# Node stage: the product with the attention weights and the adding of the constant row made by GpSimd for the edge sources

## The reference

```python
edge_index = jnp.stack([src, dst])
x = _layernorm(x + _L0_gnn_ref(x, node_vec, edge_weight, ..., edge_index), axis=-1)
x = _layernorm(x + _L1_gnn_ref(x, L1_gnn_W1, ..., L1_gnn_b3, edge_index), axis=-1)
x = _layernorm(x + _L2_gnn_ref(x, edge_attr_128, src, dst, ...), axis=-1)
x = _layernorm(x + _L3_gnn_ref(x, edge_attr_2, src, dst, ...), axis=-1)
```

```python
z2 = jnp.concatenate([h[src], h[dst], ex], axis=1)
a = jax.nn.leaky_relu(z2 @ w_attn.T, negative_slope=0.01)[:, 0]
```

## Time and profile before

| | |
|---|---|
| time, median of 3 runs | 3603.18 us (3602.86 to 3603.41) |
| the profiled execution: its time | 3606.04 us |
| its span in the trace | 3604.0 us |
| busy over the whole span | PE 2523.9 us, DVE 2602.9 us, ACT 2013.2 us, POOL 2052.6 us |
| node stage, 1200 to 1500 us (edge sources) | PE 220.80, DVE 289.52, ACT 250.32, POOL 103.11 us of 300 |
| node stage, 1550 to 1700 us (nodes without edges) | PE 132.77, DVE 136.38, ACT 140.97, POOL 57.90 us of 150 |

### The profile page before, as it was taken

One profiled execution on the slowest core, in us unless ns is written; L12 is line 12 of the kernel. 1 busy time (PEld: TensorE's weight loads), 2 busy tenths in 40 slices (PEclk: granted clock), 3 DMA queues, 4 the chain that ended last, 5 costly groups with the idle time before them and its releaser, 6 DMA issues. The chain is left out here.

```text
span 3604.0 us, 57246 instructions
## 1 busy us (share of the span) xinstructions
PE 2523.9 (70%) x14627; PEld 1907.0 (53%) x14627; DVE 2602.9 (72%) x7782; ACT 2013.2 (56%) x5963; POOL 2052.6 (57%) x1978
## 2 busy tenths in 40 slices
PE   5377744999476777697687787777767757877430
PEld 2133322666355565575466666555557757776430
DVE  8689963444597899998366677798868759878542
ACT  0034322777222888798466677688867748865110
POOL 7767774774000433342777577577467767710776
PEclk9799986999799988999899899888889979987555
DMA  3455557776299444432566677677589879933221
GB/s 94 106 147 153 154 151 165 248 243 205 86 328 273 141 147 147 135 92 77 174 212 199 190 244 247 217 239 240 181 252 269 241 237 290 284 121 112 86 89 42
DMA packets 521868, 653.93 MB, mean 181 GB/s; under 512 B 99208, under 2 KB 292294, under 8 KB 521544
## 3 DMA queue, kind: packets, MB, share of 16 engines
q1 hardware_dynamic: 455242, 548.98, 48.8%
q0 software_dynamic: 65856, 100.90, 10.3%
q10 hardware_dynamic: 446, 0.40, 0.0%
HBM read 436.87 MB, written 241.92 MB: 188 GB/s over the span
## 5 line engine op out<-in xcount | busy, mean ns | idle before, releaser
L1620 POOL DMA_INDIRECT look<-table_d,ids x196 | 196.1, 1000 | 603.8 <-DVEq L1596 559.7
L1945 POOL DMA_INDIRECT xg_c<-r_d,src_row x392 | 410.9, 1048 | 167.9 <-issue 117.1
L2703 POOL DMA_INDIRECT out<-x_f,out_row x196 | 202.9, 1035 | 177.3 <-DVE x_f L2769 118.5
L1945 POOL DMA_INDIRECT xg_c<-x1d_d,src_row x196 | 216.8, 1106 | 104.8 <-issue 59.5
L1945 POOL DMA_INDIRECT xg_c<-x2d_d,src_row x196 | 203.5, 1038 | 113.0 <-issue 59.2
L925 POOL DMA_INDIRECT xd<-in_x,ids x196 | 217.6, 1110 | 71.0 <-issue 51.7
L1945 POOL DMA_INDIRECT xg_c<-g1d_d,src_row x196 | 204.7, 1044 | 79.6 <-issue 59.5
L554 POOL DMA_INDIRECT rows_d<-row,slot_i x196 | 194.1, 990 | 69.4 <-issue 55.8
L2059 ACT ACTIVATE term_c<-xg_c,scale 128x128 f32<-128x128 f32 x392 | 125.1, 391 | 181.3 <-DMA xg_c<-x1d_d,src_row 107.6
L1964 DVE TENSOR_TENSOR_SCAN agg_t_c<-flags_c,agg_t_c,term_t_c 128x512 f32<-128x512 bf16 x96 | 122.9, 1281 | 104.7 <-ACT term_t_c L2043 59.9
L1964 DVE TENSOR_TENSOR_SCAN agg_t_c<-flags_c,agg_t_c,t_ps_c 128x512 f32<-128x512 bf16 x144 | 183.2, 1273 | 1.0 <-PE t_ps_c L2366 1.0
(11 more groups left out here) (483 smaller groups left out, 8896.0 us busy)
## 6 DMA issues: line engine op xcount, KB each, us to landing
flags_c<-cont_d SPq DMA_DIRECT2D x245, 128.0 KB, 4.4
xm<-rows_d SPq DMA_DIRECT2D x49, 512.0 KB
m_d<-m_c SPq DMA_DIRECT2D x98, 256.0 KB
r_d<-r_c SPq DMA_DIRECT2D x98, 256.0 KB
m_in_c<-m_d SPq DMA_DIRECT2D x98, 256.0 KB
e_c<-rows_d SPq DMA_DIRECT2D x98, 256.0 KB
x_f<-in_x SPq DMA_DIRECT2D x67, 256.0 KB, 4.9
out<-x_f SPq DMA_DIRECT2D x67, 256.0 KB
```

The costliest lines, as they stand in the source:

```text
L1620: pool.indirect_dma_start(out=look[:, t, :], out_offset=None, in_=table_d[:, :], in_offset=bass.IndirectOffsetOnAxis(ap=ids[:, 0, t:t + 1] ...
L1945: pool.indirect_dma_start(out=xg[:, s, k, :], out_offset=None, in_=table, in_offset=bass.IndirectOffsetOnAxis(ap=src_row[:, t:t + 1], axis=0),
L2703: pool.indirect_dma_start(out=out[:, :], out_offset=bass.IndirectOffsetOnAxis(ap=out_row[:, t:t + 1], axis=0), in_=x4[:, n % SF, k, :], in ...
```

## The change

Both steps leave DVE's code for the groups of edge sources. A new function `dense_pool` makes them on POOL: in iteration `it` first `y2` of group it-2, then `dotw` of group it-7, then the two or three indirect transfers as before. `dotw` gets a second buffer. The sum `dotk` stays on DVE, but moves to the next iteration, behind `x1`, with a wait for POOL's `attended` ahead of it and a wait for its own end behind it. Other new waits keep the buffers safe: DVE waits for `attended` three groups back ahead of `u`, and for `y2_ready` two groups back ahead of `x1`; POOL waits for `x1`, for the readers of the old `y2`, for `u` and for `dotk` two groups back.

```diff
@@ -1315,7 +1315,7 @@
             lk = sb("lk_n", [P, 2, K, D], F32, st)
             x2s = sb("x2s_n", [P, 2, K, D], F32, st)
             g1o = sb("g1o_n", [P, 2, K, D], F32, st)
-            dotw = sb("dotw_n", [P, K, D], F32, st)
+            dotw = sb("dotw_n", [P, 2, K, D], F32, st)
             dotk = sb("dotk_n", [P, 2, K], F32, st)
             x4 = sb("x4_n", [P, 3, K, D], F32, st)
             ss1 = sb("ss1_n", [P, K], F32, st)
@@ -1339,6 +1339,7 @@
             y2_ready, turned_y, yt_ready, squared_2 = signal("y2_ready"), signal("turned_y"), signal("yt_ready"), signal("squared_2")
             made_2, sloped_g, g1_ready, made_3, leaked, halved = (signal(s) for s in ("made_2", "sloped_g", "g1_ready", "made_3", "leaked", "halved"))
             summed_2, added_u = signal("summed_2"), signal("added_u")
+            attended, attended_sum = signal("attended"), signal("attended_sum")
             spread_ok, rooted_n, inv_ready, normed = signal("spread_ok"), signal("rooted_n"), signal("inv_ready"), signal("normed")
             x2s_ready, turned_g, g1o_ready = signal("x2s_ready"), signal("turned_g"), signal("g1o_ready")
 
@@ -1517,18 +1518,16 @@
                     dve.tensor_scalar(rest[:, :], ss2[:, g % 5, :], factor / D, factor * EPS, ALU.mult, ALU.add).then_inc(own.one(), 1)
                     if g >= GROUPS + 3:
                         dve.wait_ge(normed.sem, normed.at(g - GROUPS - 2))
+                    if g >= 3 and edge(g - 3):
+                        dve.wait_ge(attended.sem, attended.at(g - 2))
                     dve.wait_ge(halved.sem, halved.at(g + 1))
                     dve.tensor_tensor(u[:, g % 3, :, :], y2[:, g % 6, :, :], half_u[:, :, :], ALU.add).then_inc(added_u.sem, 1)
                     dve.wait_ge(added_u.sem, added_u.at(g + 1))
                     for k in range(K):
                         dve.bn_stats(stats[:, k, :], u[:, g % 3, k, :]).then_inc(own.one(), 1)
-                    if edge(g):
-                        dve.tensor_tensor(dotw[:, :, :], u[:, g % 3, :, :], a0[:, :, :], ALU.mult).then_inc(own.one(), 1)
                     done()
                     for k in range(K):
                         dve.bn_aggr(moments[:, g % 2, k, :], stats[:, k, :]).then_inc(own.one(), 1)
-                    if edge(g):
-                        dve.tensor_reduce(dotk[:, g % 2, :], dotw[:, :, :], AX.X, ALU.add).then_inc(own.one(), 1)
                 if 1 <= it < NG + 8:
                     dve.wait_ge(rooted_n.sem, rooted_n.at(it))
                     dve.reciprocal(inv[:, now, :, :], spread[:, was, :, :]).then_inc(own.one(), 1)
@@ -1537,9 +1536,12 @@
                 if 0 <= g < GROUPS:
                     if g >= 2:
                         dve.wait_ge(s_out[g % 2].sem, s_out[g % 2].at(g // 2))
+                        dve.wait_ge(y2_ready.sem, y2_ready.at(g - 1))
                     dve.tensor_tensor(x1[:, g % 2, :, :], nm_ps[g % 2][:, :].rearrange("p (k d) -> p k d", k=K),
                                       inv[:, now, 0, :].unsqueeze(2).to_broadcast([P, K, D]), ALU.mult).then_inc(x1s_ready.sem, 1)
                 elif GROUPS <= g < NG:
+                    if g == GROUPS:
+                        dve.wait_ge(y2_ready.sem, y2_ready.at(GROUPS))
                     dve.wait_ge(squared_2.sem, squared_2.at(g - 5))
                     if g - 6 < GROUPS:
                         dve.wait_ge(x2s_ready.sem, x2s_ready.at(g - 5))
@@ -1549,6 +1551,9 @@
                 g = it - 8
                 if 0 <= g < NG:
                     if edge(g):
+                        dve.wait_ge(attended.sem, attended.at(g + 1))
+                        dve.tensor_reduce(dotk[:, g % 2, :], dotw[:, g % 2, :, :], AX.X, ALU.add).then_inc(attended_sum.sem, 1)
+                        dve.wait_ge(attended_sum.sem, attended_sum.at(g + 1))
                         dve.scalar_tensor_tensor(shift[:, g % 2, :], moments[:, g % 2, :, 0], a_sum[:, 0:1], dotk[:, g % 2, :], ALU.mult, ALU.subtract).then_inc(own.one(), 1)
                     else:
                         dve.scalar_tensor_tensor(shift[:, g % 2, :], moments[:, g % 2, :, 0], -1.0, inv[:, now, 1, :], ALU.mult, ALU.mult).then_inc(own.one(), 1)
@@ -1558,13 +1563,6 @@
                 g = it - 4
                 if 0 <= g < GROUPS:
                     dve.tensor_copy(inv_2[:, g % 4, :], inv[:, now, 2, :]).then_inc(own.one(), 1)
-                g = it - 2
-                if 0 <= g < GROUPS:
-                    if g >= 6:
-                        dve.wait_ge(squared_2.sem, squared_2.at(g - 5))
-                        dve.wait_ge(x2s_ready.sem, x2s_ready.at(g - 5))
-                    dve.wait_ge(x1s_ready.sem, x1s_ready.at(g + 1))
-                    dve.tensor_tensor(y2[:, g % 6, :, :], x1[:, g % 2, :, :], b3_mid[:, :, :], ALU.add).then_inc(y2_ready.sem, 1)
                 if 1 <= it < NG + 8:
                     done()
                     dve.sem_inc(inv_ready.sem, 1)
@@ -1595,6 +1593,29 @@
                     done()
                     dve.sem_inc(spread_ok.sem, 1)
 
+            def dense_pool(pool, it):
+                g = it - 2
+                if 0 <= g < GROUPS:
+                    pool.wait_ge(x1s_ready.sem, x1s_ready.at(g + 1))
+                    if g >= 6:
+                        pool.wait_ge(squared_2.sem, squared_2.at(g - 5))
+                        pool.wait_ge(x2s_ready.sem, x2s_ready.at(g - 5))
+                        pool.wait_ge(added_u.sem, added_u.at(g - 5))
+                    pool.tensor_tensor(y2[:, g % 6, :, :], x1[:, g % 2, :, :], b3_mid[:, :, :], ALU.add).then_inc(y2_ready.sem, 1)
+                g = it - 7
+                if 0 <= g < GROUPS:
+                    pool.wait_ge(added_u.sem, added_u.at(g + 1))
+                    if g >= 2:
+                        pool.wait_ge(attended_sum.sem, attended_sum.at(g - 1))
+                    pool.tensor_tensor(dotw[:, g % 2, :, :], u[:, g % 3, :, :], a0[:, :, :], ALU.mult).then_inc(attended.sem, 1)
+                if 1 <= it < NG:
+                    pool.wait_ge(spread_ok.sem, spread_ok.at(it))
+                    for t in range(TILES * (it - 1) // (NG - 1), TILES * it // (NG - 1)):
+                        pool.indirect_dma_start(
+                            out=look[:, t, :], out_offset=None, in_=table_d[:, :],
+                            in_offset=bass.IndirectOffsetOnAxis(ap=ids[:, 0, t:t + 1], axis=0),
+                            bounds_check=TABLE - 1, oob_is_err=False).then_inc(looked.sem, 16)
+
             with ExitStack() as ps, nc.Block() as block:
                 nx_ps, ny_ps = bank(ps, "nx_ps"), bank(ps, "ny_ps")
                 nm_ps = [bank(ps, f"nm_ps{s}") for s in range(2)]
@@ -1614,13 +1635,8 @@
 
                 @block.gpsimd
                 def _(pool):
-                    for it in range(1, NG):
-                        pool.wait_ge(spread_ok.sem, spread_ok.at(it))
-                        for t in range(TILES * (it - 1) // (NG - 1), TILES * it // (NG - 1)):
-                            pool.indirect_dma_start(
-                                out=look[:, t, :], out_offset=None, in_=table_d[:, :],
-                                in_offset=bass.IndirectOffsetOnAxis(ap=ids[:, 0, t:t + 1], axis=0),
-                                bounds_check=TABLE - 1, oob_is_err=False).then_inc(looked.sem, 16)
+                    for it in range(NG + LAG):
+                        dense_pool(pool, it)
                     pool.wait_ge(looked.sem, looked.at(TILES))
 
                 @block.tensor
@@ -1645,7 +1661,7 @@
             retire([(s, NG) for s in (turned_x, xt_ready, made_1, squared_1, y2_ready, turned_y, yt_ready, squared_2, made_2,
                                       g1_ready, made_3, leaked, halved, summed_2, added_u)])
             retire([(looked, TILES), (setup, 1), (spread_ok, NG + 7), (rooted_n, NG + 7), (inv_ready, NG + 7), (normed, NN)])
-            retire([(s, GROUPS) for s in (sloped_g, x1s_ready, x2s_ready, turned_g, g1o_ready)])
+            retire([(s, GROUPS) for s in (sloped_g, x1s_ready, x2s_ready, turned_g, g1o_ready, attended, attended_sum)])
             retire([(x_in[s], len(range(s, NG, 6))) for s in range(6)] + [(x4_out[s], len(range(s, NN, 3))) for s in range(3)])
             retire([(group[s], shares(s, 2)) for group in (s_out, x2_out, g1_out) for s in range(2)])
 
```

## The result

The changed kernel takes 3640.86 us in the median of four runs (3633.29 to 3648.56), the kernel before 3603.3 (3602.86 to 3604.27): a ratio of 1.0104 (95% interval 1.0086 to 1.0122), slower by 1%. The forecast was 3637 us. The profiled execution took 3648.56 us, with a span of 3645.7 us against 3604.0, so 41.7 us are to be found in its trace.

A forecast was written before the change was run, and what follows sets the result against it. DVE was taken to bound the changed groups at 7.25 us an iteration; with POOL's holds 8.02 us, 0.77 more in 44 iterations, +34 us on the median 3603.2: 3637 us, 0.9% slower, range 3586 to 3676.

The forecast's parts named there:

- The bound and the gain: Edge-source groups: DVE bounds at 7.25 us an iteration; moving the steps saves 0.83 us, 37 us over 44 iterations without holds.
- The hold: POOL's reads and DVE's steps with two SBUF inputs exclude each other; the later waits, making 8.02 us an iteration; chance 0.66.
- The first case: `shift` and `spread` slip in between POOL's two steps and `attn_in` waits for both: a period of 7.76 us.
- the middle: Period of 8.02 us taken between 7.76 and 8.28, 0.77 us more than before, +34 us over 44 iterations.
- the other case: `shift` itself waits for both of POOL's steps, 0.52 us on top: a period of 8.28 us.
- The ends of the stretch: Iterations 2 to 6, only `y2` moved, at most +2.5 us; 51 to 55, only `dotw` moved, -2.4 us; they cancel.
- (a): Rival: POOL's steps don't hold DVE; period 6.42 us, -37 us, 3567 us; chance 0.18.
- (b): Rival: POOL's reads come in pieces, each tiny DVE step waits a part; period 7.22 us, 3602 us; chance 0.08.
- (c): Rival: POOL's steps take 1.54 us or more, from a heavier two-input loop; +69 us, 3672 us; chance 0.08.

The follow-up runs named there:

- both orders: Changed kernel with POOL making `dotw`, one transfer, then `y2`, and DVE's tiny steps ahead of `x1`, `dotk` ahead of the variances: period 6.00 us, ratios 0.9926 and 0.9916.

## Why the prediction was right

**The bound and the gain.** DVE as the bound and the 7.25 us held. From the first L1527 to the first L1530 it is 0.91 us after, as worked out.

**The hold.** It decided, as forecast, and the indirect evidence of the earlier trace rows was enough for its sign: POOL held by a step of DVE to the hundredth, DVE held by POOL's read for 0.05 us. Both steps of POOL do hold DVE. Who slips through was left open: 7.76 us if `shift` and `spread` pass between POOL's steps, 8.28 if `shift` waits for both. The first case is the one that came, in all iterations of the regular pattern.

**What was off.** The victim of `dotw` is the copy, which has one input, and not `attn_in`; with the copy gone it is `attn_in` (the sum in place of the copy), so the end is nearly the same, but for the 0.18 us from the end of `dotw` to `attn_in`, in which the copy ends and is waited for: `attn_in` starts 3.44 us behind `x1`, where I had POOL done at 3.17. The other 0.09 of that 0.27 is POOL's: a start at 0.78 instead of 0.89 (it started 0.09 us behind the end of `x1`, not 0.2), but steps of 1.26 us, 1.22 apart, instead of 1.14. From `attn_in` to the next `x1` it is 4.72 instead of 4.59. That makes 3.44 + 4.72 = 8.16 us. The case that came true was costed at 7.76, 0.40 too little, and its own sum would have been 3603 + 44 x 0.51 = 3626 us. The forecast took the middle, 8.02, since nothing showed who wins, and half of the other case's extra wait, which did not come, happened to stand for most of what the right case lacked. So the sign and the mechanism were foreseen; that the number is as near as it is, is in part luck. Against the middle, 43 periods (the forecast counted 44) cost 39.2 us instead of 34. The ends of the stretch, which I let cancel, cost 0.3 + 1.9 us: the nodes' part needs 196.7 us instead of 194.8. (The estimate from the GPSIMD Engine Reference in the Trainium skill, section 3.1, was 1.12 us for the step; the trace has 1.26, and the measurement decides.)

**The sum.** 3640 us on the profiled basis against 3648.6, 3637 against the median of 3640.9. The changed kernel's profiled run lies 7.7 us above its median, so the error is 4 to 9 us. The profile names 7.5 of them: 39.2 + 0.3 + 1.9 makes the 41.5 us of the stage, but for rounding, where the forecast had 34.

**The rivals.** (a), that POOL's steps hold nobody, falls with the durations of `shift` and the copy. (b), pieces, falls too: the holds end with POOL's steps. (c) was right in its direction, by 0.12 us a step. Neither the forecast nor a rival asked whether the same steps at other moments would cost less; both orders show that they do.

## What to carry to other kernels

Before work goes from VectorE to GpSimd, list what VectorE does in the microsecond in which GpSimd reads. In these traces a step there with two SBUF inputs (0.21 to 0.74 us), a copy within SBUF (0.16 to 1.24) or a step with one SBUF input and constants (0.20 to 0.58) waited to the end of GpSimd's instruction, although it had only 4 elements a partition. Put GpSimd's steps beside statistics, sums and steps with an input in PSUM. Here the iteration went from 0.91 us more than before to 0.91 less with the same spread of the transfers, and to 1.25 less with two in each, part of it by VectorE's own new order. The tell-tale in a trace is a tiny step with the duration of a large one, on an engine that looks busy.

## What the runs showed that was not expected

- A step of 4 elements took up to 2.98 us. In that iteration of the changed kernel a transfer came late, and `shift` was held through both of POOL's steps and didn't pass between them:

```profile
1517.90 1.00 POOL L1614 DMA_INDIRECT look<-table_d,ids  x1 [3.16 <-issue]
1518.46 2.98 DVE L1557 SCALAR_TENSOR_TENSOR shift_n<-moments_n,a_sum,dotk_n 128x4 f32<-128x4 f32 x1
1518.92 1.27 POOL L1604 TENSOR_TENSOR y_n<-x_n,b_mid 128x512 f32<-128x512 f32 x1
1520.14 1.27 POOL L1610 TENSOR_TENSOR dotw_n<-u_n,a 128x512 f32<-128x512 f32 x1
```

- A wait that is already fulfilled is not free on DVE. With the wait for `attended` ahead of `u` the way from `rest` to `u` is 0.19 us, as in this kernel with all on DVE,

```profile
1537.28 0.16 DVE L1518 TENSOR_SCALAR rest_n<-ss_n 128x4 f32<-128x4 f32 x1
1537.47 0.69 DVE L1524 TENSOR_TENSOR u_n<-y_n,half_u 128x512 f32<-128x512 f32 x1
```

and in the kernel with `y2` alone on POOL and in the kernel before, which don't have that wait, 0.12: about 0.07 us for one more wait.
